# A fused macaron layer on one core: the middle layernorm's statistics taken in the first expert layer's loop, and one reordering on TensorE

## The reference

```python
x = x + 0.5 * ffn(layernorm(x))      # first expert layer
x = x + attn(layernorm(x))           # 16 heads of width 8, causal, rotary positions
x = x + 0.5 * ffn(layernorm(x))      # second expert layer, same weights

def ffn(x):   # x: (4, 1024, 128), 8 experts, hidden width 512
    probs = softmax(x @ Wr + br); gates = max(probs); idx = argmax(probs)
    xn = layernorm(x) * ln_g + ln_b
    h = relu(xn @ W1[idx] + b1[idx])
    return (h @ W2[idx] + b2[idx]) * gates
```

## Time and profile before

| | us |
|---|---|
| median of 3 runs | 920.0 (919.34 to 925.11) |
| the profiled execution, its own time | 914.48 |
| its span in the profile | 912.7 |
| TensorE busy | 793.7 (87%) |
| VectorE busy | 610.1 (67%) |
| ScalarE busy | 507.5 (56%) |
| GpSimd busy | 314.0 (34%) |

### The profile page before, as it was taken

How to read it: one execution, slowest core, us unless ns; L and a number is a source line. 1 busy time by engine, 2 the same in 40 slices (tenths; PEclk the granted TensorE clock), 3 DMA queues, 4 the chain that set the end, 5 groups by cost and what they waited for, 6 DMA issues and landing times. The chain is left out here.

```text
span 912.7 us, 17879 instructions
## 1 busy us (share of the span) xinstructions
PE 793.7 (87%) x5590; PEld 444.6 (49%) x5590; DVE 610.1 (67%) x1919; ACT 507.5 (56%) x1229; POOL 314.0 (34%) x603
## 2 busy tenths in 40 slices
PE   9868889599799999999999999999999977668795
PEld 7757779355423333333333333333333336667685
DVE  4625456589766777877887788778787508544463
ACT  2135545276126776676667666766676761145462
POOL 5154644157311232223222322232223310344643
PEclk9759889799858999999999999999999988789998
DMA  9511111316531330222023302320230000311100
GB/s 305 204 42 28 42 30 33 102 44 174 140 60 18 54 51 12 46 54 53 15 41 55 54 15 40 55 53 15 41 54 2 2 30 3 118 36 31 44 31 27
DMA packets 31574, 51.46 MB, mean 56 GB/s; under 512 B 7552, under 2 KB 23296, under 8 KB 30080
## 3 DMA queue, kind: packets, MB, share of 16 engines
q1 hardware_dynamic: 24880, 40.84, 19.5%
q0 software_dynamic: 4096, 8.50, 3.5%
q10 hardware_dynamic: 2512, 1.06, 0.5%
HBM read 35.20 MB, written 14.78 MB: 55 GB/s over the span
## 5 line engine op out<-in xcount | busy, mean ns | idle before, releaser
L1441 DVE CUSTOM_DVE_ANT_0 cst<-psS,mask_row 128x768 bf16<-128x768 f32 (+7 forms) x512 | 364.7, 755 | 103.6 <-PE psS L1298 101.2
L1405 ACT ACTIVATE prob<-psST 128x512 f32<-128x512 f32 (+3 forms) x750 | 317.4, 496 | 162.4 <-PE psST L1329 158.8
L1343 PE MATMUL a_psO<-prob,vs 128*32 128x512 f32 (+3 forms) x1536 | 166.7, 506 | 2.8 <-ACT prob L1405 1.7
L1525 POOL TENSOR_TENSOR a_gate<-a_zeros 1x1 f32<-1x1 f32 x128 | 23.4, 183 | 334.2 <-ACT prob L1405 334.2
L1329 PE MATMUL psST<-a_qs,ks 75*128 75x512 bf16 (+1 forms) x480 | 123.7, 327 | 5.9 <-ACT prob L1405 3.5
L1298 PE MATMUL psS<-ks,a_qs 72*128 72x512 bf16 (+2 forms) x480 | 118.8, 337 | 5.9 <-DVE a_rowmax L1441 5.7
L767 POOL DMA_INDIRECT tok<-rows,f_there_number x64 | 61.5, 961 | 104.7 <-DVE f_number L488 43.1
L716 ACT ACTIVATE f_xnT<-f_ps_half,gb 128x128 f32<-128x128 f32 x64 | 29.3, 457 | 107.6 <-PE f_ps_half L644 62.6
L1298 PEld LDWEIGHTS psS<-ks,a_qs 72*128 72x128 bf16 x480 | 35.6, 99 | 101.4 <-DVE a_rowmax L1441 33.3
L653 PE MATMUL f_ps_wide<-f_xnT,f_w1s 128*128 x312 | 56.5, 309 | 32.6 <-issue 20.4
L521 DVE TENSOR_SCALAR f_hidT<-f_ps_wide,f_w1s 128x128 f32<-128x128 f32 x156 | 47.3, 345 | 52.7 <-remote 32.5
(11 more groups left out here) (183 smaller groups left out, 1088.3 us busy)
## 6 DMA issues: line engine op xcount, KB each, us to landing
a_qs<-q_split SPq DMA_DIRECT2D x60, 96.0 KB
rows<-tok SPq DMA_DIRECT2D x8, 524.0 KB, 4.2
ks<-k_split SPq DMA_DIRECT2D x32, 128.0 KB
qs<-q_split SPq DMA_DIRECT2D x36, 96.0 KB
q_split<-p_part SPq DMA_DIRECT2D x24, 128.0 KB, 2.4
k_split<-p_part SPq DMA_DIRECT2D x24, 128.0 KB, 2.4
ks<-k_split SPq DMA_DIRECT2D x16, 192.0 KB
w<-in_Wb SPq DMA_DIRECT2D x1, 2064.0 KB, 7.9
```

The lines of the kernel that those rows point to most:

```text
L1343: last = nc.tensor.matmul(psO[32 * h:32 * h + 32, c0:c0 + w], vs[r][:, j, h, :], prob[:, u % RING, h, 0:w], start=(j == 0), stop=(u + 1 in ...
L1405: nc.scalar.activation(prob[:, u % RING, h, 0:w], score_buffer(s, u * QH + h)[:, 0:w], ACT.Exp, scale=SCALE).then_inc(exp_done, 1)
L1441: last = nc.vector.tensor_tensor_reduce(out=out[:, a * CH:a * CH + width], in0=ps[:, a * CH:a * CH + width], in1=mask_row[:, S - width:], ...
```

## The change

- `n.tok` becomes 134 floats wide; the six numbers of `bn_stats` have columns 128 to 133. The tile `n.stats` is gone. The three scalars share columns 128 to 130 with the statistics once these have been used. In the sorted copies `rows` stays 131 floats wide, and its stores now read 524 B out of rows of 536 B.
- In the first layer's loop VectorE runs `keep_stats(t)` behind `add_x`: it waits for that addition and for the gate, then takes `bn_stats` of the finished tile into the tile's own last columns. GpSimd's scatter of tile t waits for this, and moves 134 floats of a row. `x_after_first` is 134 wide.
- The reload fetches whole rows of 134 floats, contiguous on both sides. `measure` is gone, `scales` reads the statistics out of `n.tok`.
- TensorE's order at the start of the projection becomes turn 0, products 0, turn 1, turn 2, products 1, turn 3, products 2 and so on.

```diff
--- before.py
+++ after.py
@@ -37,7 +37,9 @@
 NCH = S // CH
 CB = CH // P
 SCALE_AT, OFFSET_AT, HALF_GATE = D, D + 1, D + 2
-TW = D + 3
+SW = D + 3
+STATS = 6
+TW = D + STATS
 W1W, W2W = F + FB, FB * D + D
 LR, XR, VALUES = 12, 16, 4
 LATE = E - 1
@@ -181,7 +183,6 @@
         n.w1 = sb("w1", [P, E, W1W])
         n.w2 = sb("w2", [P, E, W2W])
         n.mean = sb("mean", [P, NT])
-        n.stats = sb("stats", [P, NT, 6])
         n.shared = sb("shared", [P, NT, D])
         n.vals = sb("vals", [P, NST, TB, RW])
 
@@ -195,8 +196,8 @@
 
         n.q_dram = nc.dram_tensor("q_split", (KINDS * DK, NCH, B * H, CH), BF16, kind="Internal").ap()
         n.k_dram = nc.dram_tensor("k_split", (KINDS * DK, B * H, S), BF16, kind="Internal").ap()
-        n.rows_dram = [nc.dram_tensor(f"rows{r}", (B * S, TW), F32, kind="Internal").ap() for r in range(2)]
-        n.x_dram = nc.dram_tensor("x_after_first", (B * S, D), F32, kind="Internal").ap()
+        n.rows_dram = [nc.dram_tensor(f"rows{r}", (B * S, SW), F32, kind="Internal").ap() for r in range(2)]
+        n.x_dram = nc.dram_tensor("x_after_first", (B * S, TW), F32, kind="Internal").ap()
 
 
         def sem(name):
@@ -330,7 +331,7 @@
             sem(k) for k in ("table_read", "tiles_found", "low_made", "slots_found", "numbers_done", "numbers_ready",
                              "experts_known"))
         loaded = [sem(f"loaded{i}") for i in range(LR)]
-        rows_written = sem("rows_written")
+        rows_written, stats_kept = sem("rows_written"), sem("stats_kept")
         x_normed, x_turned, x_ready, w1_ready, h_done, h_low, h_high, y_done, y_biased, gated, y_ready = (
             sem(k) for k in ("x_normed", "x_turned", "x_ready", "w1_ready", "h_done", "h_low",
                              "h_high", "y_done", "y_biased", "gated", "y_ready"))
@@ -389,12 +390,12 @@
                             last_ = nc.vector.tensor_tensor(x, x, both[:, :, 0:D], ALU.add)
                         last_.then_inc(added, 1)
                         dve.wait_ge(added, g + 1)
-                    link.then(nc.vector.bn_stats(n.stats[:, t, :], n.tok[:, t, 0:D]))
+                    link.then(nc.vector.bn_stats(n.tok[:, t, D:], n.tok[:, t, 0:D]))
                 link.join()
 
             def scales():
 
-                even, odd, sq_even, sq_odd = (n.stats[:, :, k] for k in (1, 4, 2, 5))
+                even, odd, sq_even, sq_odd = (n.tok[:, :, D + k] for k in (1, 4, 2, 5))
                 sm, var, diff = total[:, :], spread[:, :], corr[:, 0, :]
                 sh, ro, co = shift[:, :, :], root[:, :, :], corr[:, :, :]
                 link.then(nc.vector.tensor_tensor(diff, even, odd, ALU.subtract))
@@ -544,6 +545,13 @@
                     nc.vector.scalar_tensor_tensor(x, yb[i % 2][:, :], gate[:, i % 2:i % 2 + 1], x,
                                                    ALU.mult, ALU.add).then_inc(y_ready, 1)
 
+            def keep_stats(t):
+                if tile_there(t):
+
+                    dve.wait_ge(y_ready, t + LATE + 1)
+                    dve.wait_ge(gated, t + LATE + 1)
+                    nc.vector.bn_stats(row[:, t, D:D + STATS], row[:, t, 0:D]).then_inc(stats_kept, 1)
+
             def step(i):
                 if item(i):
                     values(mybir.EngineType.DVE, item_expert, i, E - 1, expert)
@@ -552,6 +560,8 @@
                 weigh(i - 1)
                 normalise(i + 2)
                 add_x(i - 1)
+                if r == 0:
+                    keep_stats(i - 1 - LATE)
                 own_gate(i)
 
             run(step)
@@ -752,7 +762,7 @@
             sp.wait_ge(rows_ready, 3)
             for b in range(B):
                 sp.dma_start(n.rows_dram[r].rearrange("(p n) d -> p n d", p=P)[:, b * TB:(b + 1) * TB, :],
-                             n.tok[:, b * TB:(b + 1) * TB, :]).then_inc(rows_stored, 16)
+                             n.tok[:, b * TB:(b + 1) * TB, 0:SW]).then_inc(rows_stored, 16)
 
         @block.gpsimd
         def _(pool):
@@ -765,7 +775,7 @@
                 if tile_there(t):
                     wait(pool, x_normed, t - LR + 1)
                     pool.indirect_dma_start(
-                        out=row[:, t, :], out_offset=None, in_=n.rows_dram[r][:, :],
+                        out=row[:, t, 0:SW], out_offset=None, in_=n.rows_dram[r][:, :],
                         in_offset=bass.IndirectOffsetOnAxis(ap=there_number[:, t:t + 1],
                                                             axis=0)).then_inc(loaded[t % LR], 16)
 
@@ -773,11 +783,14 @@
                 if tile_there(t):
                     if r == 1 and t == 0:
                         pool.wait_ge(numbers_ready, 2)
-                    pool.wait_ge(y_ready, min(t + LATE, NS - 1) + 1)
+                    if r == 0:
+                        pool.wait_ge(stats_kept, t + 1)
+                    else:
+                        pool.wait_ge(y_ready, min(t + LATE, NS - 1) + 1)
                     pool.indirect_dma_start(
                         out=target, out_offset=bass.IndirectOffsetOnAxis(
                             ap=number[:, t:t + 1], axis=0),
-                        in_=row[:, t, 0:D], in_offset=None, bounds_check=B * S - 1,
+                        in_=row[:, t, 0:TW if r == 0 else D], in_offset=None, bounds_check=B * S - 1,
                         oob_is_err=False).then_inc(rows_written, 16)
 
             for i in range(-GATHER_AHEAD, NS + 1):
@@ -870,16 +883,9 @@
     def _(dve):
         link = Chain(dve, chain)
 
-        def measure(first, last):
-            for b in range(first, last):
-                dve.wait_ge(x_back[b], 16)
-                for t in range(b * TB, (b + 1) * TB):
-                    link.then(nc.vector.bn_stats(n.stats[:, t, :], n.tok[:, t, 0:D]))
-            link.join()
-
         def scales(first, last):
             sl = slice(first * TB, last * TB)
-            sm, sp, ro, co, st = total[:, sl], spread[:, sl], root[:, sl], corr[:, sl], n.stats[:, sl, :]
+            sm, sp, ro, co, st = total[:, sl], spread[:, sl], root[:, sl], corr[:, sl], n.tok[:, sl, D:]
             link.then(nc.vector.tensor_tensor(co, st[:, :, 1], st[:, :, 4], ALU.subtract))
             link.then(nc.vector.tensor_tensor(sp, st[:, :, 2], st[:, :, 5], ALU.add))
             link(nc.vector.tensor_tensor(sm, st[:, :, 1], st[:, :, 4], ALU.add))
@@ -918,7 +924,8 @@
                                     ALU.subtract).then_inc(lo_done[0], 1)
 
         for first, last in GROUPS:
-            measure(first, last)
+            for b in range(first, last):
+                dve.wait_ge(x_back[b], 16)
             scales(first, last)
         for g in range(NC8):
             rotate(g, g % 2)
@@ -960,11 +967,12 @@
         pe.wait_ge(n.weights_loaded, 16 * LOADS)
         nc.tensor.matmul(psP[1][1][:, 0:E], n.shared[:, 0, :], n.wrc[:, :], start=True, stop=True).then_inc(n.router_turned, 1)
         turn(0, 0)
+        products(0, 0)
         turn(1, 1)
-        for g in range(NC8):
+        for g in range(1, NC8):
+            if g + 1 < NC8:
+                turn(g + 1, (g + 1) % 2)
             products(g, g % 2)
-            if g + 2 < NC8:
-                turn(g + 2, g % 2)
 
     @block.scalar
     def _(act):
@@ -1056,7 +1064,7 @@
     def _(sp):
         sp.wait_ge(n.scattered, 16 * NT)
         for b in range(B):
-            sp.dma_start(n.tok[:, b * TB:(b + 1) * TB, 0:D],
+            sp.dma_start(n.tok[:, b * TB:(b + 1) * TB, :],
                          n.x_dram.rearrange("(p n) d -> p n d", p=P)[:, b * TB:(b + 1) * TB, :]).then_inc(x_back[b], 16)
 
         def keep(g, k):

```

## The result

The changed kernel takes 933.1 us in the median (925.9 to 935.1, 4 runs) where the kernel before took 919.7 (915.1 to 925.1, 4 runs) on the same chip: a ratio of 1.018, interval 1.012 to 1.025. The profiled execution took 932.8 us with a span of 931.0, against 914.5 and 912.7. The kernel before took 865 to 925 us in the sets of runs that the experiments belong to (chip 9 gave 918.6 in one set and 865.8 in another), so times are compared by their ratio to it within one set. The profile of the stores-only kernel (e2) is of a disturbed execution; its ratio rests on others.

A forecast was written before the change was run, and what follows sets the result against it. It took a chain ahead of a full VectorE in the projection, and TensorE at the loop's end, as bounds. +0.8 + 0.5 + 0.4 - 1.1 = +0.6 us gave 915.1 profiled, 920.6 median; own range 916 to 925, whole 914 to 927.5.

The forecast's parts named there:

- Row stores late: Rival: row stores 7 us later than the old reload delay both layers' gathers, 8 us slower, 928.6 us; chance 0.09.
- Covered. The row stores ... Taken at 0: Row stores in 524 B pieces land 9.9 us after first issue, before the first gathers, so they cost 0.
- Within 1%: 0.88: Whole kernel: chance 0.88 that the time stays within 1% of before, between 910.8 and 929.2 us.
- VectorE in the loop: Expert loop: statistics add 0.42 us per step, hidden in ordinary steps; steps with register loads cost 0.8 and 0.5 us.
- The sum of 0.8, 0.5 and 0.4 for loop and tail: Loop and last scatter: 0.8 us for two load steps, 0.5 for steps 32 and 36, 0.4 for the tail.
- VectorE did not become the bound: Rival: VectorE bounds the expert loop and each of 32 steps pays, up to 13.4 us, 932.3 us; chance 0.06.
- The stall: VectorE waiting for something outside the records may come or go: taken at 0, with 2.6 us to either side.
- The reload: Start of the projection: first batch of whole rows lands 3.8 us after issue instead of 4.4, 0.6 us gained.
- The projection: Products 0 start 4.6 us earlier, but turn 2 waits for normalise 2, so rotate 1 gains 1.1 us.
- The term of 5.4 us for their length: Products 0 on TensorE: four of eight passes at half clock, 5.4 us; bounds 3.60 and 7.2.
- the first gathers wait for the row stores: Sign against the forecast: it is wrong if this happens, or if rotate 1 moves by more than 3 us.

The follow-up runs named there:

- e2: The kernel before with only the rows' pitch in SBUF changed to 536 B, so stores go out in 524 B pieces: ratio to before 1.025.
- e5: e3 with bare DMA groups behind its end, stores and loads of varied piece and pitch: 524 B stores at multiples of 524 took 18.3 us, at 768 10.7.
- e9: The kernel before, unaltered, for a second profile: first row store at 32.9 us, last scatter to rotate 1 in 26.56 us.
- e10: The kernel before with only TensorE's new order of products and turns: ratio to before 1.000, last scatter to rotate 1 27.41 us.
- e8: The changed kernel, unaltered, run again beside e6 on the same chip: ratio to before 1.018.
- e6: e1 with ScalarE normalising chunk 2 before it copies turned chunk 1: ratio to before 1.000.
- e7: The changed kernel with row stores and gathers of 512 B at a 512 B pitch, output not the reference's: 924.3 us once, beside 925.5 for before.
- e1: The changed kernel with whole rows of 134 floats stored and gathered in both layers: ratio to before 0.997.
- e3: e1 with TensorE's order at the start of the projection as before: ratio to before 0.997.
- e4: e3 with the statistics taken in the projection as before: ratio to before 0.997.
- e12: e3 unaltered, for a second profile: ratio to before 0.990, last scatter to rotate 1 23.77 us.

## Why the prediction was wrong

It said 920.6 us, and the chance of slower by over 1% was 0.09. The measured 933.1 is the case it called *Row stores late*.

- **The step that failed is "Covered. The row stores ... Taken at 0".** It took the old reload, with nearly the same length of pieces in the other direction, as the price of the new stores: last landing 9.9 us after the first issue. Measured: the first gathers, which wait for that landing, go 19.05 and 19.77 us after the first issue. The reload's pieces were 512 bytes at multiples of 512 in DRAM, which e5's L244 shows to be fast as a store too; the new ones start at multiples of 524. The row that it leant on differed in two things, direction and start, and it corrected for neither; by e5 either alone would have cost nothing (8.8 and 9.8 us), and both together cost 18.3. With 10.22 us of cover for a priced 9.9 the margin was 0.3 us, so an error of 3% in an estimate from another direction already broke it.
- **The rival had the right mechanism and too small a price.** It gave 7 us of lateness in each layer and took off 2.9 us of cover and 1.5 more in each, so 8 us in all. Measured: 8.83 and 9.51 us. The cover was there at the first xnT (1.8 and 4.9 us), but from the gather on the layers took 1.52 and 1.05 us longer, not less. In the first layer that says little, since the same code varies by 4.2 us there. In the second the runs disagree: from the first gather to the end the changed kernel took 126.47, and kernels with the stores of before 125.42 (before), 126.50 (e9) and 127.39 (e10), so no cover is seen; but on the chip of e8 it took 127.34 where e6 and e7, with early stores, took 130.21 and 131.82. How much of the cover arrives stays open. And at 928.6 the rival lay inside "Within 1%: 0.88", so the 0.09 for a loss of over 1% did not hold it at all.
- **VectorE in the loop.** 0.42 us per step was predicted, 0.32 measured: the gap behind the addition is 0.04 and not 0.13, the statistics take 0.294, more than the 0.206 per piece of a row of eight, and the gate starts before they end. The sum of 0.8, 0.5 and 0.4 for loop and tail stands against 0.6 to 1.1 (e1, e3 against e4): right in kind, somewhat high. VectorE did not become the bound.
- **The stall.** It allowed 2.6 us to either side for an engine that waits for something outside the records. In the loop of the first layer the kernel before has 12 such waits, 42.7 us in sum over the engines, and the changed kernel 13 and 48.2. The same code differs by 4.2 us in that loop (before against e9), within the 5.2 between the two sides, so the size was fair, though it is the sum of many stalls and not one.
- **The reload.** 3.8 predicted from issue to the first landing, 3.8 in the after profile: the scales start 3.84 us after the issue.
- **The projection.** Products 0 were to start 4.6 us earlier relative to the last scatter, and did. The term of 5.4 us for their length was mis-sized: 6.40, at a granted clock of 0.57, so mostly at the lower level, and within the bounds of 3.60 and 7.2. From there each step came as written: ScalarE's wait, turn 2 behind normalise 2, VectorE idle for over 4 us. So 0.15 us was left of 1.1. That the reordering itself gives nothing was in the prediction; that it costs 0.9 to 1.9 us (e1 against e3, e10) was not, since it was never priced against the old order with the statistics gone.
- **Not foreseen at all**: the stretch with the attention is 6.4 us shorter in the changed kernel's profiles, and the clock in 15 us of it differs; that the change causes this is not shown. The medians' difference, 13.4 us, is near 18.3 (stores) + 1.5 + 1.1 (loops) - 0.15 - 6.4 = 14.4, the table without its first line. As four of these five terms also vary between executions of the same code, the nearness is no proof.
- The sign that the prediction named for itself, "the first gathers wait for the row stores", is what the trace shows.

The version that the experiments point to is e3: whole rows stored and gathered, loop statistics, the old order on TensorE. By the ratios to before it is about 2% faster than the changed kernel; against the kernel before it is 0.3% (12 runs, the interval reaches 1) or 1.0% (4 runs) faster. By time it can't be told from e1 and e4 (0.997 each); only the traces put it 1.9 us ahead of e1, and level with e4.

## What to carry to other kernels

When an edit turns a contiguous store into pieces, look first at where each piece starts in DRAM; storing the few unused columns too was worth 2% here. A price taken from a transfer in the other direction is no price: where cover is as thin as 0.3 us, the bounds of such a term belong into the range. And when work is moved forward on one engine, price the new order against the old order of the changed kernel, not only against the kernel before: an engine that got its input earlier may be waiting for the one behind it.

## What the runs showed of the hardware that I had not expected

- A store of 4096 pieces of 512 bytes from SBUF to DRAM takes 8.8 us at starts of multiples of 512 and 18.3 at multiples of 524; loads take 9.7 us at multiples of 512 and 9.8 at multiples of 524. In the changed kernel's first layer the DMA engines were busy from 38 to 50 us and moved 124 to 137 GB/s, as in this window (the last three numbers are clock, DMA share and GB/s):

```profile
38.00:42.00 4.00, 3.04 (x37) 2.89 (x35) 3.96 (x8) 1.15 (x1) 0.00 (x0) 0.93 1.23 124
```

The share near or above 1 says that the engines are occupied, not that they move much. The Trainium skill (DMA: Bandwidth & Descriptors, section How a descriptor splits into AXI transactions) describes what a start off a 256-byte boundary costs on the side that is read: bytes below the start are fetched and not used. The loads here don't show it, 9.8 us against 9.7. The cost that the runs do show is in stores, and its boundary is a smaller one: of the multiples of 576 only every fourth is a multiple of 256, and those pieces take 9.5 us against 8.8.
- TensorE's clock in the same stretch of the same code was 0.67 in one run and 0.50 in another. In the attention's opening 15 us ran at 0.89 to 0.96 in six profiles and at 0.50 to 0.57 in the eight others; the same code up to there (e3, e12 against e5) came out both ways.
- The expert loop has two lengths that the code does not set. From first gather to last scatter it took 117.4 to 126.8 us in the eight profiles from sets of runs in which the kernel before takes about 920 us, and 92.2 to 95.5 us in the six from the sets in which it takes 865. In the eight, engines waited 10 to 15 times in that stretch for something outside the records (`remote`), 42 to 57 us in sum over the engines; in the six there is no such wait. Chip 9 has given both. What the engines wait for stays open.
